# A two-stage decoder layer in split fp32: another order of work for the first batch at the seam of the stages

## What is computed

```python
x = layernorm(x + attn(x))               # first stage of the kernel
x = layernorm(x + xattn(x, ctx, mask))   # "x2": quantised x times quantised ctx[b], plus mask
x = layernorm(x + ffn(x))                # gated MLP 512->2048->512, plus 8 looked-up experts a token

def xattn(x, weight, bias):
    x_dq, w_dq = fp8_quant_dequant(x), fp8_quant_dequant(weight)   # scale by the tensor's absmax
    return einsum('bmk,bkn->bmn', x_dq, w_dq) + bias
```

## Time and profile before

| | |
|---|---|
| three runs | 818.97, 819.68 (median), 821.32 us |
| the profiled execution | 818.65 us, of which the span from first to last instruction is 816.8 us |
| busy in the span | TensorE 778.0 us (95%), VectorE 675.2 (83%), GpSimd 372.9 (46%), ScalarE 314.6 (39%) |
| DMA | 81.69 MB |
| granted TensorE clock, mean | 0.979 |

### The profile page before, as it was taken

One profiled execution on the slowest core, in us unless ns is written; L12 is line 12 of the kernel. 1 busy time (PEld: TensorE's weight loads), 2 busy tenths in 40 slices (PEclk: granted clock), 3 DMA queues, 4 the chain that ended last, 5 costly groups with the idle time before them and its releaser, 6 DMA issues. The chain is left out here.

```text
span 816.8 us, 10532 instructions
## 1 busy us (share of the span) xinstructions
PE 778.0 (95%) x3537; PEld 636.2 (78%) x3541; DVE 675.2 (83%) x1331; ACT 314.6 (39%) x688; POOL 372.9 (46%) x303
## 2 busy tenths in 40 slices
PE   8999999989578999999999999999999999999995
PEld 6878878878456778888888888888877877878784
DVE  6887678887797883177779999999999999999997
ACT  6444236354554322212353333333433333333322
POOL 1332122242232320212478667676666667667432
PEclk9999999999869999999999999999999999999998
DMA  8577504635496243000022231322332333222113
GB/s 321 220 147 169 97 7 110 168 87 94 55 297 149 69 118 128 26 1 32 29 76 86 77 97 41 106 80 67 96 102 82 96 93 109 65 87 71 39 54 153
DMA packets 51334, 81.69 MB, mean 100 GB/s; under 512 B 17519, under 2 KB 26479, under 8 KB 50768
## 3 DMA queue, kind: packets, MB, share of 16 engines
q0 software_dynamic: 24384, 33.48, 19.3%
q1 hardware_dynamic: 25312, 47.52, 16.8%
q10 hardware_dynamic: 1584, 0.01, 0.1%
HBM read 110.44 MB, written 12.58 MB: 151 GB/s over the span
## 5 line engine op out<-in xcount | busy, mean ns | idle before, releaser
L1697 PE MATMUL gu<-x_hi,w_hi 128*128 128x512 f32 x528 | 207.7, 393 | 3.1 <-DVE mid L1467 1.7
L1698 PE MATMUL gu<-x_lo,w_hi 128*128 128x512 f32 x528 | 206.2, 390 | 0.0
L1699 PE MATMUL gu<-x_hi,w_lo 128*128 128x512 f32 x528 | 206.1, 390 | 0.0
L1216 POOL TENSOR_TENSOR h_lo<-mid,h_hi 128x512 fp32r<-128x512 f32 x62 | 80.1, 1313 | 106.9 <-ACT h_hi L1336 106.4
L1697 PEld LDWEIGHTS gu<-x_hi,w_hi 128*128 128x128 f32 x528 | 99.6, 189 | 26.5 <-DVE mid L1467 4.2
L1346 ACT ACTIVATE gates<-dots 128x1 f32<-128x1 f32 x144 | 29.3, 203 | 232.0 <-DVE dots L1558 232.0
L1699 PEld LDWEIGHTS gu<-x_hi,w_lo 128*128 128x128 f32 x528 | 99.5, 188 | 20.9
L1698 PEld LDWEIGHTS gu<-x_lo,w_hi 128*128 128x128 f32 x528 | 99.6, 189 | 20.3
L1235 POOL DMA_INDIRECT ctx_q<-table_dram,row_i x64 | 80.3, 1255 | 62.3 <-DVE xall L1567 42.6
L1235 POOL DMA_INDIRECT scratch<-table_dram,row_i x64 | 82.6, 1291 | 39.5 <-issue 21.4
L1697 PE MATMUL ob<-w_hi,h_hi 128*128 128x512 f32 x248 | 97.4, 393 | 2.9 <-POOL h_lo L1216 2.9
(11 more groups left out here) (210 smaller groups left out, 1383.8 us busy)
## 6 DMA issues: line engine op xcount, KB each, us to landing
stage<-in_ctx SPq DMA_DIRECT2D x7, 1024.0 KB, 6.2
total<-prod POOLq DMA_DIRECT2D x12, 512.0 KB, 4.7
xall<-half_bo POOLq DMA_DIRECT2D x4, 1024.0 KB, 10.1
xhat<-in_L_ffn_gate_w SPq DMA_DIRECT2D x8, 512.0 KB, 3.4
xhat<-in_L_ffn_up_w SPq DMA_DIRECT2D x8, 512.0 KB, 3.6
xall<-in_mask_Bx1xS_ff POOLq DMA_DIRECT2D x4, 1024.0 KB, 10.8
xhat<-in_L_ffn_down_w SPq DMA_DIRECT2D x8, 512.0 KB, 3.6
x_dram<-xall SPq DMA_DIRECT2D x4, 1024.0 KB, 6.7
```

The source lines that it names most:

```text
L1216: nc.gpsimd.tensor_tensor(lo[:, c], mid[c][:], hi[:, c].bitcast(F32), ALU.subtract).then_inc(hlo_done, 1)
L1697: nc.tensor.matmul(dst, lhs[0], rhs[0], start=start, stop=False)
L1698: nc.tensor.matmul(dst, lhs[0], rhs[1], start=False, stop=False)
L1699: return nc.tensor.matmul(dst, lhs[1], rhs[0], start=False, stop=stop)
```

## The change

For batch 0 alone the statistics of x2 are made in another way. VectorE's residual also gives the row sum (`accum_out`), a one-column instruction makes minus the mean of it, and ScalarE squares tile plus minus-mean with the sum of squares as second output. The variance comes from that sum. `normalise` adds minus-mean and multiplies. The x2 transposes of batch 0 go to the banks `ob` (the cross banks) instead of `gu`. TensorE alternates: transposes of a tile of batch 1, cross product of a tile of batch 0. ScalarE does two tiles of `scaled(1)` ahead of the squares and two behind `high_x2(0)`. The low parts of blocks 2 and 3 move from GpSimd to VectorE: block 2 behind `middle(0, 0)`, block 3 at the end of unit 0; GpSimd waits for both before it splits block 4. SyncE issues the two copies to `table_dram` behind the last store of x2, and the load of the last row behind the next load.

```diff
@@ SyncE @@
                 load(3, 0, 3)
-                sp.dma_start(table_dram[:, 0:D], down_embed).then_inc(table_in, 16)
-                sp.dma_start(table_dram[:, D:2 * D], up_embed).then_inc(table_in, 16)
                 store_x2(0)
...
                 store_x2(3)
-                sp.wait_ge(table_in, 32)
-                sp.dma_start(last_row[:], table_dram[NE - 1].partition_broadcast(P)).then_inc(row_in, 16)
+                sp.dma_start(table_dram[:, 0:D], down_embed).then_inc(table_in, 16)
+                sp.dma_start(table_dram[:, D:2 * D], up_embed).then_inc(table_in, 16)
@@ GpSimd @@
                 add_mask(1)
-                pool.wait_ge(l2_done, TB)
-                low_w(2, 0, 2, 0)
-                low_w(3, 0, 3, 1)
...
                     if n + 1 < TB:
+                        if n == 0:
+                            pool.wait_ge(wlo_done, 4)
                         low_w(load_index(1, n), 1, n, load_index(1, n) % 2)
@@ ScalarE @@
+                def deviation(i):
+                    act.wait_ge(minus_first, i + 1)
+                    if i:
+                        act.wait_ge(squared, i)
+                    nc.scalar.activation(junk2[:], tile(i), ACT.Square, bias=z_minus[:, i:i + 1], accum_out=z_square[:, i:i + 1]).then_inc(squared, 1)
...
-                scaled(1, range(TB))
+                scaled(1, (0, 1))
+                for i in range(TB):
+                    deviation(i)
                 for n in range(TB - 1):
                     high_x2(n)
                     if n == 0:
+                        scaled(1, (2, 3))
@@ VectorE @@
+                def first_residual(i):
+                    dve.wait_ge(cross_mm, i + 1)
+                    dve.wait_ge(xm_in[0], 16)
+                    own.did(nc.vector.scalar_tensor_tensor(tile(i), ob[i][:], unscale[:], tile(i), ALU.mult, ALU.add, accum_out=z_sum[:, i:i + 1]))
+                    own.wait()
+                    nc.vector.tensor_scalar(z_minus[:, i:i + 1], z_sum[:, i:i + 1], -1.0 / D, None, ALU.mult).then_inc(minus_first, 1)
+                def first_variance(k):
+                    cols = slice(2 * k, 2 * k + 2)
+                    dve.wait_ge(squared, 2 * k + 2)
+                    nc.vector.tensor_scalar(var2[:, cols], z_square[:, cols], 1.0 / D, LN_EPS, ALU.mult, ALU.add).then_inc(v3_ready, 1)
+                def first_normalise(i):
+                    dve.wait_ge(r3_ready, i // 2 + 1)
+                    nc.vector.tensor_scalar(tile(i), tile(i), z_minus[:, i:i + 1], rstd2[:, i:i + 1], ALU.add, ALU.mult).then_inc(x2_done, 1)
+                def first_low_w(m, r, slot):
+                    dve.wait_ge(whi_done, m + 1)
+                    hi, lo = parts(0, r)
+                    nc.vector.tensor_tensor(flat(lo, r), stage_of(r, slot), flat(hi, r).bitcast(F32), ALU.subtract).then_inc(wlo_done, 1)
...
-                residual(0, (0, 1))
-                variance((0, 1))
-                residual(0, (2, 3))
-                variance((2, 3))
-                normalise(0, (0, 1))
-                normalise(0, (2, 3))
+                for i in range(TB):
+                    first_residual(i)
+                first_variance(0)
+                first_variance(1)
+                for i in range(TB):
+                    first_normalise(i)
                 low_x2(0)
...
                     middle(n, 0)
+                    if n == 0:
+                        first_low_w(2, 2, 0)
...
                         quantise(n + 2, (3,))
+                        if n == 0:
+                            first_low_w(3, 3, 1)
@@ TensorE @@
-                cross(0, nothing)
-                transposes(1, range(TB), own_bank, x1t_mm, freed(y_done, 0))
-                transposes(0, range(TB), own_bank, x2t_mm, freed(y_done, TB), x2_done)
+                for i in range(TB):
+                    transposes(1, (i,), own_bank, x1t_mm, freed(y_done, 0))
+                    cross(0, nothing, (i,))
+                x2_transposes(0, nothing)
```

More of the change, by code:

```diff
@@ L1699, in three, with x2_transposes, transposes @@
                     return nc.tensor.matmul(dst, lhs[1], rhs[0], start=False, stop=stop)
-                def transposes(b, tiles, bank, count, free, ready=None):
+                def x2_transposes(b, free):
+                    for i in range(TB):
+                        free(i)
+                        pe.wait_ge(x2_done, TB * b + i + 1)
+                        for c in range(KC):
+                            j = TB * b + i
+                            last = nc.tensor.transpose(x2t_bank(b, i)[:, c * P:(c + 1) * P], xall[:, j * D + c * P:j * D + (c + 1) * P], ident[:])
+                        last.then_inc(x2t_mm, 1)
+                def transposes(b, tiles, bank, count, free):
                     for i in tiles:
                         free(i)
-                        if ready is not None:
-                            pe.wait_ge(ready, TB * b + i + 1)
                         for c in range(KC):
@@ L1710, in transposes, with cross @@
                         last.then_inc(count, 1)
-                def cross(b, free):
-                    for i in range(TB):
+                def cross(b, free, tiles=range(TB)):
+                    for i in tiles:
                         free(i)
@@ L1798, in _ @@
                         gate_up(n, 0, n, 1, None)
-                    down_early(n, 0, freed(z2_done, TB * (n + 1)))
-                    transposes(n + 1, range(TB), own_bank, x2t_mm, x2_bank_free(n), x2_done)
+                    down_early(n, 0, freed(z2_done, TB * n))
+                    x2_transposes(n + 1, x2_bank_free(n))
                     down_early(n, 1, nothing)
```

32 lines of the change are left out of this document (21 added, 11 removed).

## The result

Medians, each beside the kernel before on the same chip:

| | kernel before | changed kernel |
|---|---|---|
| time | 820.39 us (818.97 to 822.33, 5 runs) | 814.54 us (812.22 to 816.27, 5 runs) |
| profiled execution, span | 818.65 us, 816.8 us | 816.27 us, 814.5 us |
| granted clock, mean | 0.979 | 0.981 |

The account below looks back on a forecast made before the run. TensorE, busy 95% of the span, was taken as the bound. Gains of 1.5 and 2.45 us less 0.25, given as 3.95, took 818.65 to 814.75 profiled, 815.8 from the median; forecast 816.0, range 813.3 to 819.3.

Parts of the forecast that it names:

- Place one: Chain from batch 0's quantiser to the first gate product: new statistics and TensorE order were to gain 1.5 us.
- residual spacing: VectorE's batch 0 residuals, without bn_stats but with the accumulator's read: starts 0.95 us apart.
- last residual: VectorE's fourth residual of batch 0: to start at 230.8 us, against 232.56 before.
- clock does not fall: Rival between last cross product and x2 transposes: clock stays up, another 3.2 us saved, 812.8 us; chance 0.07.
- The rival that the clock stays low up to 230.3: Alternating transposes and cross products: late clock rise leaves the quantiser-to-gate chain no gain, 817.2 us; chance 0.13.
- the 226.87: Time in us when the clock was to rise from 0.50 to 1.00 again, during the cross products.
- Place two: End of unit 0: later table copies let batch 1's mask land early; 2.45 us of gaps less 0.25 left.
- mask in by the time it was needed: Batch 1's mask, issued at 233.7, was to take 11 to 13 us and land by 247.
- Block 2 on the path: Low part of weight block 2, moved to VectorE behind `middle` in unit 0: costs 1.21 us before batch 1's residuals.
- these were called hidden: VectorE's slow quantiser steps, one of 2.75 us: hidden behind gate products, so losing them is worth nothing.
- The rival of GpSimd holding up block 2: VectorE's block 2 in unit 0, slowed by GpSimd's `low_h`: 2.0 us more, 817.8 us; chance 0.05.

Follow-up runs that it names:

- e2_tables_early: Changed kernel with the two table copies issued in their old early place; 820.69 us, ratio 1.0006 to the kernel before.
- e6_early_filled: Changed kernel with early table copies and ten idle TensorE products ahead of batch 1's x2 transposes; 820.84 us, ratio 1.0004.
- e5_only_tables_late: Kernel before with only the two table copies and the last row's load issued later; 815.02 us, ratio 0.9933.
- e3_split_on_gpsimd: Changed kernel with the low parts of weight blocks 2 and 3 back on GpSimd; 812.95 us, ratio 0.9905.
- e12_fast_all: Changed kernel with blocks 2 and 3 split on GpSimd and idle TensorE products in waits between the stages and two first-stage waits; 808.80 us, ratio 0.9870.
- e4_bn_stats_again: Changed kernel with batch 0's statistics by bn_stats on VectorE again, without ScalarE's squares; 815.01 us, ratio 0.9928.
- e1_after_again: Changed kernel unchanged, measured and traced again beside the kernel before; 814.28 us, ratio 0.9912.
- e9_before_second: Kernel before, unchanged, measured and traced a second time; 820.18 us, ratio 1.0003.

## Why the prediction was right and where it was off

The forecast of faster, its 816.0 us and its range were right: 814.5 lies in the range. Where the time comes from was seen less well than the sum suggests.

- **Place one, forecast 1.5 us, came out at 1.56 where the x2 transposes start, and at 2.3 for the first gate product** (seam + 18.99 before, 16.65 after). The steps held: residual spacing 0.87 and 0.94 without a wait, where 0.95 was taken (the accumulator's read is 0.08, as taken); last residual at 231.03 on the old scale (230.8), scaling at 232.94 (232.9), x2 transposes at 233.54 (233.6). The wait on the last cross product was 0.35, since the clock rose at seam + 7.0 instead of 5.7. What was missed stands behind the transposes: they took 2.88 us, not 3.64, as their first part still ran at full clock. That is 0.8 us, a quarter of the rival "clock does not fall", and it is luck: the unchanged kernel has 3.08 in its second trace. Over the traces the x2 transposes start at seam + 13.9 in all four with the old chain and at 12.0 to 12.6 with the new one and its order; the first gate product comes at 18.1 to 19.0 and at 16.5 to 16.8 (the clock left to itself). So place one is worth 1.3 to 2.5 us there, by where the clock falls in an execution.
- **The rival that the clock stays low up to 230.3** did not come. The Trainium skill (TensorE: Matmul & The Clock Gate, PE-mode transpose) was read as making it the likelier course. In the alternating order the rise came at seam + 5.7 to 7.4 in six traces. With all cross products first it came at seam + 5.7 to 8.8 in five. So the 1.3 us between the earlier trace rows and the changed kernel can't be put down to the order, and the 226.87 that the prediction built on was one execution's. No run here isolates transposes, so what they count for is open.
- **Place two, forecast 2.4 us, came out at 2.25 between the first two traces** (late down products 4.59 sooner in all, less 2.34). Its steps held: mask in by the time it was needed, residual at 247.23 on the old scale (248.1), one gap of 0.54 left. The prediction's split doesn't add up: 1.5 and 2.45 less 0.25 are 3.7, not 3.95. The missing 0.25 is real: sixteen x2 transposes without a break take 1.91 us, where two groups of eight took 1.08 and 1.09. But the price of this place was taken from one execution, and that was where the prediction failed in size. The earlier trace rows gave 17.4 us for the mask. Over the four traces with early copies and this mask (two of before, e2_tables_early, e6_early_filled) it was 17.4, 18.6, 19.6 and 19.8. The one in hand was the shortest. In the second trace of before the same place ended 2.5 us later still, and the end 3.3 later, a fallen clock behind the gap included. From the seam to the end the change thus wins 4.2 us against the first trace of before and 7.4 against the second, the longest of its twelve executions; the 5.85 between medians lies between them. The sum of 3.9 was priced on an execution with an early mask. That this one was luckier than most is likely from these four landings and not shown by more.
- **Which edit bears the gain.** The prediction put 1.5 us on place one and 2.4 on place two as if they added. By the medians the late copies alone bring 6.0 (e5_only_tables_late), and the rest of the change without them nothing that can be told (e2_tables_early): what place one wins, VectorE spends waiting for the mask, 5.41 us instead of 3.76. Only once the mask is early can the statistics count, and then for 0.7 between medians and 1.9 between traces, part of the latter clock. Between e5_only_tables_late and the change it is 0.5 to 0.7 between medians and 0.9 from the seam (592.4 and 591.5), in place of the 1.5 that the sum gave to place one. This is the term that failed: the places don't add.
- **Block 2 on the path, 1.21 us**, was a correct duration (1.22) and the wrong balance. Left on GpSimd the blocks slow VectorE's quantiser steps to 2.77 and 1.75, and these were called hidden. They are hidden no longer once the gate products end sooner. The two prices nearly cancel: medians 814.28 and 812.95, and 812.01 and 812.18 with the clock kept up.
- **The rival of GpSimd holding up block 2** did not come: 1.22 us on VectorE, beside the 1214 ns of the earlier trace rows. The Trainium skill (GPSIMD Engine Reference, Specifications) has the engines contend when VectorE reads two SBUF inputs. The slow quantiser steps of e3_split_on_gpsimd agree, with 2.77 us for a step of 0.69, while `low_h`, which started at 248.81 under the end of block 2, did it no harm; that `low_h` took 1.51 us itself, where it took 1.29 in e3_split_on_gpsimd with nothing of the kind beside it.
- **Late in the kernel** the change gives a little back. From the first routing product to the end it takes 481.07 us, where before took 480.68 in both its traces. This 0.3 to 0.4 us is in all kernels with the rest of the change (480.9 to 481.2), in e5_only_tables_late it is 0.1; where it arises wasn't looked into.

Open: why the mask's landing varies from 17.4 to 19.8 us under the copies; how much of the 6 us is clock and how much the wait itself (the mean granted clock was 0.9817 over the six executions of e5_only_tables_late and 0.9793 over those of before beside it; that is some 4 us less at 0.50 in an execution, and at the 0.53 of e12_fast_all some 2 us of time, an estimate); and the share of the statistics.

## What to carry to other kernels

A DMA's landing time under contention is a spread, not a number: if a term of the sum rests on one transfer that shares its time with large copies, get it from a second execution, or give it a range. The same holds for the moment at which the clock rises or falls: here it moved by 3 us against the program. Large copies with a late consumer belong after the transfers that the next stage waits for, and two `dma_start` moved were here all of the gain that the medians can tell. Before shortening a chain, ask what else its consumer waits for (here a mask); and where TensorE waits 2 us and runs at half clock afterwards, idle products in the wait gave 3.4 us in the first stage and about 2.3, with intervals that overlap, around the seam.

## What the hardware showed that was not expected

- The granted clock fell to 0.50 behind waits of TensorE of only 1.81 us (before its product at 116.78) and 2.24 us (before 177.33) in the changed kernel, but not always: the same waits were followed by no fall near 117 us in e4_bn_stats_again and e6_early_filled, and by none near 177 in e1_after_again and e9_before_second. In e12_fast_all, with idle products in the two waits, it stayed at 1.00. The kernel before had 3.4 us at 0.50 near 117 us in one execution and 6.8 in another.
- With the clock at 1.00 from the start to the last few microseconds, as traced in e12_fast_all, the kernel's time scattered by 0.6 us in six runs.
- The four masks are of one size (1024 KB); beside the copies the one of batch 1 took 17.4 to 19.8 us and the other three 9.3 to 11.4. Without the copies beside it that one took 11.7 in the changed kernel and 12.4 in e5_only_tables_late.
- An accumulating residual took VectorE 0.74 to 0.75 us, as a plain one does, and its read 0.08 us more; the accumulating square took ScalarE 0.72 + 0.19 us.
